# An audio tower's token stage: the embedding's bias added by VectorE, gamma and beta one step later, ScalarE's squares read from SBUF

## What is computed

```
y = patches @ W.T + b                       # embedding, 256 wide
h = (y - mean(y)) * rsqrt(var(y) + eps) * gamma + beta
h = h + attention(layernorm(h))             # one head, 124 tokens of one sequence
h = h + moe(layernorm(h))                   # router (softmax, top 2 of 6), three-layer experts
```

## Time and profile before

| | us |
|---|---|
| median of 3 runs | 1243.38 (1239.12 to 1246.04) |
| the profiled execution | 1241.32 |
| its span | 1239.5 |
| TensorE busy | 1182.3, 95% |
| VectorE busy | 982.0, 79% |
| ScalarE busy | 887.6, 72% |
| GpSimd busy | 885.7, 71% |
| mean granted TensorE clock | 0.987 of full speed |

### The profile page before, as it was taken

How to read it: one execution, slowest core, us unless ns; L and a number is a source line. 1 busy time by engine, 2 the same in 40 slices (tenths; PEclk the granted TensorE clock), 3 DMA queues, 4 the chain that set the end, 5 groups by cost and what they waited for, 6 DMA issues and landing times.

```text
span 1239.5 us, 28038 instructions
## 1 busy us (share of the span) xinstructions
PE 1182.3 (95%) x7784; PEld 1050.0 (85%) x7784; DVE 982.0 (79%) x3290; ACT 887.6 (72%) x2107; POOL 885.7 (71%) x674
## 2 busy tenths in 40 slices
PE   6999999999999999999788999999999999999994
PEld 5888988898889888888677888989988988899983
DVE  5678888888888888887698877788878887788773
ACT  4788888888888888886555675757766766666662
POOL 2227888888888788887788676766776686677666
PEclk9999999999999999999899999999999999999997
DMA  4324665454545545654489979877888788878865
GB/s 134 110 92 124 162 167 131 123 134 127 125 124 134 127 128 139 173 166 120 130 191 272 245 149 261 173 141 147 177 213 210 148 179 193 219 158 163 226 119 59
DMA packets 146471, 195.50 MB, mean 158 GB/s; under 512 B 38920, under 2 KB 104204, under 8 KB 146316
## 3 DMA queue, kind: packets, MB, share of 16 engines
q1 hardware_dynamic: 71036, 125.04, 32.9%
q0 software_dynamic: 74016, 67.88, 32.7%
q10 hardware_dynamic: 1264, 0.79, 0.2%
HBM read 162.79 MB, written 99.09 MB: 211 GB/s over the span
## 4 chain that ended last, share of the span: by engine, by line
PE 53%; ACT 11%; SPq 10%; issue 9%; DVE 7%; POOL 5%; DMA 4%; POOLq 0%; ACTq 0%; DVEq 0%
PE bank L961 17%; PE bank L752 12%; PE bank L989 8%; SPq L496 6%; POOL expert_rows L666 3%; PE bank L906 3%; PE bank L807 3%; PE bank L950 2%; PE bank L892 2%; ACT rec L1056 2%; DMA half_sb<-split_weights 2%; ACT square L1097 2%; DVE h L1372 2%; SPq L503 2%; PE bank L798 2%
## 5 line engine op out<-in xcount | busy, mean ns | idle before, releaser
L735 POOL DMA_INDIRECT out<-yo,tail x236 | 384.0, 1627 | 128.5 <-issue 71.2
L666 POOL DMA_INDIRECT expert_rows<-rec,row_i x256 | 354.1, 1383 | 78.0 <-issue 67.2
L1175 ACT ACTIVATE h2v<-bank,small 128x512 f32<-128x512 f32 x118 | 81.3, 690 | 173.8 <-PE bank L961 173.8
L989 PE MATMUL bank<-w_sb,h_hi 128*128 128x256 f32 x944 | 184.9, 289 | 3.6 <-issue 3.6
L961 PE MATMUL bank<-x_hi,w_sb 128*128 128x512 f32 x472 | 157.8, 395 | 5.5 <-DVE x_lo L1616 4.6
L961 PE MATMUL bank<-h_hi,w_sb 128*128 128x512 f32 x472 | 157.2, 394 | 3.8 <-issue 2.3
L989 PEld LDWEIGHTS bank<-w_sb,h_hi 128*128 128x128 f32 x944 | 151.7, 192 | 4.3 <-issue 4.2
L989 PE MATMUL bank<-w_sb,h_lo 128*128 128x256 f32 x472 | 133.9, 284 | 0.0
L961 PEld LDWEIGHTS bank<-x_hi,w_sb 128*128 128x128 f32 x472 | 90.0, 191 | 24.7 <-issue 4.8
L752 PE MATMUL bank<-tok_proj,xT_hi 128*124 128x256 f32 x512 | 101.3, 290 | 9.0 <-DVE tok_proj L1201 9.0
L961 PEld LDWEIGHTS bank<-h_hi,w_sb 128*128 128x128 f32 x472 | 88.8, 188 | 23.7 <-issue 4.1
(11 more groups left out here) (244 smaller groups left out, 3189.8 us busy)
## 6 DMA issues: line engine op xcount, KB each, us to landing
w_sb<-split_weights SPq DMA_DIRECT2D x165, 512.0 KB
xg<-expert_rows SPq DMA_DIRECT2D x59, 530.0 KB, 4.3
half_sb<-split_weights SPq DMA_DIRECT2D x33, 512.0 KB, 5.3
out<-h SPq DMA_DIRECT2D x32, 496.0 KB
split_weights<-half_w SPq DMA_DIRECT2D x36, 256.0 KB, 3.7
x_in<-in_x SPq DMA_DIRECT2D x32, 250.0 KB, 12.0
small<-in_esmall SPq DMA_DIRECT2D x59, 134.0 KB
raw_w<-in_eweights SPq DMA_DIRECT2D x36, 128.0 KB, 3.9
```

The costliest lines, as they stand in the source:

```text
L666: pool.indirect_dma_start(rows_dram, bass.IndirectOffsetOnAxis(ap=row_i[0:TOK, slot, j, k:k + 1], axis=0), rec[0:TOK, slot, j, :], None).t ...
L735: pool.indirect_dma_start(out, bass.IndirectOffsetOnAxis(ap=kept_tail(t)[:, j, E8:].bitcast(I32), axis=0), sums_out(t)[:, j, :], None, com ...
L989: mm = pe.matmul(banks[6 + b][:, i * D:(i + 1) * D], act[:, c, j * P:(j + 1) * P], w[:, 2, c, wh, :], start=(c == 0 and p == 0), stop=(c = ...
L1175: act.activation(h2v[:, m, 0:cols], banks[bank + m][:, 0:cols], ACT.Relu, bias=small_in(t)[:, DC + m:DC + m + 1]).then_inc(S["h2_v"], 1)
```

## The change

The embedding's bias is no longer a matmul: it is loaded to all 128 partitions as `bias_bc`, centred there, and VectorE adds it when it copies y out of PSUM. That copy (two instructions of 512 wide) moves from the end of VectorE's round to between the first statistics and the gates, and raises a new semaphore `embedded`, which now frees banks 6 and 7 for TensorE and starts ScalarE's squares. Gamma moves into h = y * rstd * gamma, and beta becomes two more instructions of 512 wide. ScalarE squares y from SBUF: two sequences before `xn1`, two between its two `v_sb` copies. `shifts` moves from behind `half_w` to right behind the gates. At the start, two clears on GpSimd, SyncE's wait for them, one of two DMAs of the bias, and the split of the bias into halves are gone. The cut diff (counts of semaphores that only shift by a constant are left out):

```diff
-        bias_row = {n: sb(f"{n}_bias", [P, D], F32R) for n in ("tok",)}
+        bias_bc = sb("tok_bias_bc", [P, D])
...
-            sp.wait_ge(S["pool_const"], 1)
-            for r in (0, 32):
-                sp.dma_start(bias_raw["tok"][r:r + 1, :], tok_b).then_inc(S["tok_bias_loaded"], 16)
+            sp.dma_start(bias_bc[:], tok_b.to_broadcast([P, D])).then_inc(S["tok_bias_loaded"], 16)
...
-            pool.memset(bias_raw["tok"][0:33, :], 0.0).then_inc(done, 1)
-            pool.memset(bias_row["tok"][:].bitcast(F32), 0.0).then_inc(done, 1)
...
-                        bank_read(pe, (S["ln1"], g - 1, (g - 1) * LN1_N + 1 + pair))
+                        bank_read(pe, (S["embedded"], g - 1, (g - 1) * 2 + 1 + pair))
                         for j in (0, 1):
                             at = (2 * pair + j) * ROWS_X
                             into = banks[6 + pair][0:TOK, j * D:(j + 1) * D]
                             for c in range(DC):
-                                product(into, [t[:, at + c:at + c + TOK] for t in (xT_hi, xT_lo)],
-                                        [proj["tok"][:, b, c, :] for b in range(2)], c == 0, False)
-                            if it == -1:
-                                pe.wait_ge(S["proj_low"], 2)
-                            mm = pe.matmul(into, ones_r[:, 0:TOK], bias_row["tok"][:], start=False, stop=True)
+                                mm = product(into, [t[:, at + c:at + c + TOK] for t in (xT_hi, xT_lo)],
+                                             [proj["tok"][:, b, c, :] for b in range(2)], c == 0, c == DC - 1)
                         mm.then_inc(S["tok_ps"], 1)
...
-                if xa:
-                    g, slot, rnd = xa
-                    wait(act, S["rstd13"], deviations(g - 2))
-                    for j in range(GB):
-                        act.wait_ge(S["tok_ps"], g * 2 + j // 2 + 1)
-                        wait(act, S["squares"], g * GB + j)
-                        act.activation(square[0:TOK, :], banks[6 + j // 2][0:TOK, (j % 2) * D:(j % 2 + 1) * D], ACT.Square,
-                                       scale=D ** -0.5, accum_out=mv[0:TOK, 0, j, 1:2]).then_inc(S["squares"], 1)
...
+                if xa:
+                    squares(xa[0], 0)
...
+                        if pair == 0 and xa:
+                            squares(xa[0], 1)
+                elif xa:
+                    squares(xa[0], 1)
+
+            def squares(g, pair):
+
+                wait(act, S["rstd13"], deviations(g - 2))
+                for j in (2 * pair, 2 * pair + 1):
+                    act.wait_ge(S["embedded"], g * 2 + 1 + pair)
+                    wait(act, S["squares"], g * GB + j)
+                    act.activation(square[0:TOK, :], y[0:TOK, j, :], ACT.Square, scale=D ** -0.5,
+                                   accum_out=mv[0:TOK, 0, j, 1:2]).then_inc(S["squares"], 1)
...
+                    if it == 0:
+                        v.wait_ge(S["const_loaded"], N_CONST)
                     for j in range(GB):
-                        v.wait_ge(S["ln1"], at + 1 + j // 2)
+                        v.wait_ge(S["embedded"], g * 2 + 1 + j // 2)
                         v.scalar_tensor_tensor(out=h[R, g % KEPT, j, :], in0=y[R, j, :], scalar=rstd[R, 0, j:j + 1],
-                                               in1=beta_bc[R, :], op0=ALU.mult, op1=ALU.add).then_inc(S["ln1"], 1)
+                                               in1=gamma_bc[R, :], op0=ALU.mult, op1=ALU.mult).then_inc(S["ln1"], 1)
+                    for pair in range(2):
+                        v.wait_ge(S["ln1"], at + 2 + 2 * pair)
+                        v.tensor_tensor(h[R, g % KEPT, 2 * pair:2 * pair + 2, :], h[R, g % KEPT, 2 * pair:2 * pair + 2, :],
+                                        beta_bc[R, :].unsqueeze(1).to_broadcast([TOK, 2, D]), ALU.add).then_inc(S["ln1"], 1)
                 if x0:
                     g, slot, rnd = x0
-                    statistics(1, lambda j: h[R, g % KEPT, j, :], S["ln1"], g * LN1_N + 2 + GB, g)
+                    statistics(1, lambda j: h[R, g % KEPT, j, :], S["ln1"], g * LN1_N + 2 + GB, (-1, -1, 0, 0))
                 if it == 0:
                     fold_weights()
                     shifts(0)
+                if xa:
+                    g, slot, rnd = xa
+                    for pair in range(2):
+                        v.wait_ge(S["tok_ps"], g * 2 + pair + 1)
+                        v.tensor_tensor(y[R, 2 * pair:2 * pair + 2, :],
+                                        banks[6 + pair][R, :].rearrange("p (b n) -> p b n", b=2),
+                                        bias_bc[R, :].unsqueeze(1).to_broadcast([TOK, 2, D]), ALU.add
+                                        ).then_inc(S["embedded"], 1)
                 if x4:
                     gates(*x4)
+                if x0 and it > 0:
+                    shifts(x0[0])
...
-                if x0 and it > 0:
-                    shifts(x0[0])
...
                     split(ORDER[0], h1v, h1_hi, h1_lo, S["h1_v"], S["h1_split"])
-                if xa:
-                    g, slot, rnd = xa
-                    at = g * LN1_N
-                    if it == -1:
-                        v.wait_ge(S["const_loaded"], N_CONST)
-                    for pair in range(2):
-                        v.wait_ge(S["squares"], g * GB + 2 * pair + 2)
-                        v.tensor_tensor(y[R, 2 * pair:2 * pair + 2, :],
-                                        banks[6 + pair][R, :].rearrange("p (b n) -> p b n", b=2),
-                                        gamma_bc[R, :].unsqueeze(1).to_broadcast([TOK, 2, D]), ALU.mult
-                                        ).then_inc(S["ln1"], 1)
```

## The result

The changed kernel takes 1250.41 us (median of 11 runs, 1247.31 to 1253.43), the kernel before beside it 1244.38 (11 runs): a ratio of 1.0051, interval 1.0036 to 1.0067. It is 6 us slower, at the upper end of my range, where I forecast no change. Its profiled execution took 1252.82 us, its span 1251.0.

A forecast was written before the change was run, and what follows sets the result against it. TensorE bounds the kernel at 17.55 us a round; a GpSimd-VectorE ring takes nearly all its gain. Terms -1.1, +1.3, -0.9 and +0.3 give -0.4 us: 1240.9 profiled, 1243.0 median, range 1230 to 1251.

The forecast's parts named there:

- The ring: Stage A: GpSimd `rstd13` through `rstd2`, then VectorE `shifts` to second statistics, and back; 17.07 us without delays, 17.51 with.
- TensorE's gain: Stage A: four bias matmuls fewer save TensorE 0.47 us a round, making its round 17.08 us.
- GpSimd's wait before `rstd13`: Sign that the forecast is right: no wait of GpSimd there but 0.2 us.
- The delays: GpSimd's DMAs end late behind VectorE instructions with two SBUF operands: 0.45 us a round taken, bounds 0 and 0.95.
- Rivals 1: TensorE keeps the round: DMAs slip between VectorE's instructions, delay 0, round 17.08 us, time 1232; chance 0.26.
- rival 2: Beta's lock slows the DMAs: 0.95 us delay, round 18.0 us, time 1255, half the loss for 0.75; chance 0.15.
- ScalarE at nothing: ScalarE's squares from SBUF may cost at most 0.6 us more a round; waits cover it, taken as 0.
- Rounds 5 to 8: Stage A: three rounds at 17.51 us where GpSimd had run at 17.08: +1.3 us.
- The start: Rounds 0 to 5: fill +0.5 us by round 2, -2.7 by round 5; GpSimd's `rstd13` of round 5 at -1.1.
- The first indirect DMA: GpSimd's first DMA comes 4.03 us late for itself and stays so; after it GpSimd sets the pace.
- The last rounds: End of stage A: the embedding is gone and the beta instructions run once more, +0.3 us.
- Stage B untouched: The second stage was to contribute no change to the total of -0.4 us.

The follow-up runs named there:

- experiment 4: Also written shift_mid: changed kernel with `shifts` behind `row_i`, between its old and new place; 1237.39 us, 0.9961 of the kernel before.
- experiment 6: Also written after_again: the changed kernel run again, letter for letter; 1249.71 us, 1.0077 of the kernel before.
- experiment 5: An extra GpSimd indirect DMA during the set-up, in the changed kernel (1244.23 us, 1.0016 of the kernel before) and in two other kernels.
- no_beta: Changed kernel without the two beta instructions, so other output and routing of tokens; 1243.94 us, 1.0005 of the kernel before.
- after: The changed kernel itself; 1250.41 us, 1.0051 of the kernel before.
- early_back: Changed kernel with `shifts` in its old place behind `half_w` in rounds 1 to 5 only; 1249.52 us, 1.0055 of the kernel before.
- shift_back: Changed kernel with `shifts` back in its old place behind `half_w`; 1250.7 us, 1.0072 of the kernel before.
- split44: Changed kernel with GpSimd's indirect DMAs of a group parted 4 and 4 instead of 5 and 3; 1254.3 us, 1.0101 of the kernel before.
- mid_warm: Changed kernel with `shifts` behind `row_i` and an extra indirect DMA during the set-up; 1231.07 us, 0.9906 of the kernel before.
- before_warm: Kernel before the change with an extra indirect DMA during the set-up; 1245.31 us, 1.0025 of the kernel before.

## Why the prediction was wrong in its result and right in its mechanism

1. *The ring*: forecast 17.51 us a round, measured 17.51 in most of the rounds from 5 on. Its terms: GpSimd 12.05 forecast, 12.10 measured; VectorE 5.24 and 5.20; the hops 0.23 and 0.22. TensorE's gain was taken by it, as I said; `shifts` waits 0.38 us for `rstd` and TensorE waits for `rec`, as said, though 0.16 us each time where I had some 0.4 a round. GpSimd's wait before `rstd13` was to be 0.2 us and is 0.51 in a common round: a ring of 17.51 leaves GpSimd, whose own round is 17.04 (experiment 4), that much idle.
2. *The delays*: third and fourth DMA late by 0.15 and 0.37 us over 1.32, where I had worked out 0.2 and 0.35. Rivals 1 (none) and 2 (0.95) are out as the price of a common round. Beta itself took 1.29 us for two, about what `xn1T_lo` takes for two, and the DMAs of these rounds were held up by the rest of one instruction of VectorE. The first DMA of round 4 was held up by both of beta's (term 5 below). The rule of the Trainium skill that stood behind rival 2 (SBUF — State Buffer, "Who interferes with whom"), an exclusive lock, fits both: the first DMA waited for beta's end, the others for the end of one instruction.
3. *ScalarE at nothing*: the squares from SBUF take 0.40 to 0.42 us instead of 0.38; hidden, as said. *Rounds 5 to 8*: forecast +1.3, measured (167.45 - 114.91) - (163.04 - 111.80) = +1.3.
4. **The start, first failed term.** I forecast `rstd13` of round 4 1.7 us sooner than before; it came 0.9 later, 2.6 us off. I had the fill at +0.5 us by round 2 and 3.2 us back by round 5, as if rounds 2 to 4 were TensorE's. `rstd13` of round 2 came 2.4 us later (59.04 after 56.64), and 1.5 came back by round 4. Two things were left out. TensorE's granted clock: beta (1.2 us) and a start of h 0.3 us later make `qk_raw` 1.5 us later, TensorE stands idle for it 4.3 us instead of 2.4, and its granted clock in the 10 us from 24 on is 0.50 (1.2 GHz throughout), where it was 0.66 (columns as in the earlier trace rows, changed kernel, then before):
```profile
24.00:34.00 10.00, 8.06 (x35) 7.38 (x36) 7.14 (x23) 7.08 (x18) 2.13 (x3) 0.50 0.43 138
```
```profile
24.00:34.00 10.00, 9.15 (x49) 8.28 (x50) 8.78 (x22) 6.71 (x17) 1.38 (x2) 0.66 0.47 147
```
From this wait to its first `xn` transposes TensorE takes 2.6 us instead of 1.9, and they start at 28.48, 2.2 us later than in the earlier trace rows. And VectorE: in round 2 TensorE's transposes are only 0.5 us late (56.88 after 56.42), but VectorE takes 13.35 us from `negmax` to the end of the second statistics, where it took 12.36. This term is read from the two traces; no run takes it apart.
5. **The first indirect DMA, second failed term**. "Comes 4.03 us late and stays so": it came 4.47 late and took 2.83 us instead of 1.56. From `rstd13` of round 4 to the next `rstd2` it was 14.07 us, now 15.76: +1.7. It repeats in this program (experiment 6) and goes with an early DMA (experiment 5). Of the 1.7, 1.27 are the DMA's length, and that is beta's doing. VectorE in the changed kernel, then the first DMA of `no_beta`:
```profile
98.90 1.29 DVE L1305 TENSOR_TENSOR h<-h,beta_bc 124x512 f32<-124x512 f32 x2
```
```profile
96.39 1.56 POOL L663 DMA_INDIRECT expert_rows<-rec,row_i  x1 [4.84 <-issue]
```
The DMA starts at 98.80, in the last h; beta ends at 100.19, and the DMA 1.44 us later. In all six builds with beta and no early DMA (`after`, `after_again`, `early_back`, `shift_back`, `split44`, `shift_mid`) it ends 1.42 to 1.44 us behind beta, whatever its start, and takes 2.69 to 2.90 us; without beta it takes 1.56 as in the kernel before. So rival 2's lock is real for this one DMA, and I had looked for it only in the common round. Why later DMAs slip in between two such instructions and this one does not is open, and so are the other 0.44 us, by which it comes later. Both failed terms together: round 5 at +3.1 instead of -1.1.
6. **Round 23, a term left out.** `choose_early` stands on VectorE between `place` and `placed`, that is, behind `shifts` in the new order: inside the ring. Round 23 takes 19.64 us, 2.13 over the others; before it took 18.46, 0.91 over 17.55, the rest being cover. `choose_early` itself lasts 2.1 us on VectorE. I listed what is queued behind the moved step for a common round and not for the one round that has more. But its place behind `shifts` is not what costs: in `shift_mid` and `mid_warm` it stands ahead of `shifts`, and round 23 takes 19.50 us, 2.45 over 17.05 (`shift_mid`, GpSimd):
```profile
405.49 0.26 POOL L652 TENSOR_SCALAR vareps<-mv 124x8 f32<-124x8 f32 x1
...
424.99 0.24 POOL L652 TENSOR_SCALAR vareps<-mv 124x8 f32<-124x8 f32 x1 [2.21 <-DVE mv L1230]
```
It is in VectorE's own loop with `rstd13` in either order (experiment 4), and the cover is gone: before, VectorE waited up to 1.56 us a round for `half_w`, in the changed kernel not at all. With three rounds 0.15 us longer and the last three 0.23 shorter, rounds 8 to 30 took 387.14 us instead of my 385.2; the kernel before 386.13.
7. *The last rounds*: +0.5, forecast +0.3. *Stage B untouched*: holds for the medians.

The sum as measured: +3.1, +1.3, +1.0, +0.5 = +6.0 us, where I had -1.1, +1.3, -0.9, +0.3. Experiment 5 tests term 5: with round 4 where it was (92.69 after 92.34), 4.7 us less in round 5 are 5.0 us less at the end of stage A. Terms 4 and 6 were not tested by a run of their own. What I also missed is the side of the risk. In the kernel paced by TensorE a late first DMA and a long single round were mostly covered (of the 2.4 us that `before_warm` takes off round 5, 0.8 are left at the end of stage A; of the 2.1 us of `choose_early`, 0.91 show); where GpSimd or a ring through it sets the pace, nothing is given back. Each of these small terms had to be priced without cover; two were priced with it, and the third was left out.

## What to carry to other kernels

When a step is moved ahead of others on one engine and waits for a second engine that in turn waits for what now stands behind it, add up the ring; compare it with the present round, and ask what the first round and the rounds that are not like the rest add to it. Look then for a place one step later: here 1 us of work ahead of `shifts` instead of behind it turned a loss of 6 us into a gain of 5, and an early first DMA added 6 more (experiments 4 and 5). Before the whole time of a kernel with altered values is read, run the old work on the same altered values.

## What was not expected of the hardware

GpSimd's first indirect DMA of the program is dear, and its price is not constant: 4.03 us late and 1.56 long before, 4.4 to 4.6 late and 2.7 to 2.9 long with beta in VectorE's way, 4.84 and 1.56 without beta, 0.22 and 1.44 if one has been done in the set-up. Later ones take 1.31 to 1.32 us (1.43 the first behind `rstd`), and more by what is left of VectorE's instruction with two operands in SBUF: 0.15 and 0.37 us here. In the other direction nothing was seen: beta's additions took 1.29 us for two with a DMA starting in the second.
